# GpSimd adds the squares of the two channel groups of layer 3's output, and TensorE multiplies the mean once instead of twice

## The reference, cut to what matters

```python
x_n  = group_norm(x)                                  # 32 groups of 8 channels
q, k, v = split(silu(x_n @ w_qkv.T))
q, k = rope(rms_norm(q, w_qn)), rope(rms_norm(k, w_kn))
wp = silu(x_n @ w_wp.T + b_wp)                        # width and sharpness of the mask
scores = (q . k over the 49 neighbours) * scale - (1 - soft_mask(wp)) * 10000
out = softmax(scores) . v over the 49 neighbours
out = out / sqrt(mean(out * out, over the 256 channels) + eps) * w_on     # the change is in this mean
x = x + silu((out + v) @ w_out.T)
```

## Time and profile before

| what | value |
|---|---|
| median of three executions | 3406.79 us (3405.43 to 3414.38) |
| the profiled execution's own time | 3416.4 us |
| its span | 3414.6 us |
| TensorE (PE) busy | 3097.6 us, 91%, 38656 products |
| VectorE (DVE) busy | 2203.3 us, 65% |
| ScalarE (ACT) busy | 2053.3 us, 60% |
| GpSimd (POOL) busy | 1155.5 us, 34% |
| mean granted TensorE clock | 0.962 of full |

### The profile page before, as it was taken

How to read it: one execution, slowest core, us unless ns; L and a number is a source line. 1 busy time by engine, 2 the same in 40 slices (tenths; PEclk the granted TensorE clock), 3 DMA queues, 4 the chain that set the end, 5 groups by cost and what they waited for, 6 DMA issues and landing times. The chain is left out here.

```text
span 3414.6 us, 93918 instructions
## 1 busy us (share of the span) xinstructions
PE 3097.6 (91%) x38656; PEld 1747.5 (51%) x38656; DVE 2203.3 (65%) x5202; ACT 2053.3 (60%) x4412; POOL 1155.5 (34%) x1446
## 2 busy tenths in 40 slices
PE   6999999999965999999999968999995899999996
PEld 2333333333313555565656536777774566666664
DVE  5877878877744667677676633545543566666664
ACT  2667666766644555556555425666562677777774
POOL 3433434343311222222212202222222555555544
PEclk9999999999986999999999989999998999999998
DMA  6777788787753233323322214445443233333332
GB/s 202 158 173 161 160 182 178 145 183 161 151 131 107 67 88 84 86 69 92 79 71 68 71 49 162 148 146 164 141 137 137 82 94 106 106 108 113 115 94 80
DMA packets 286232, 413.93 MB, mean 121 GB/s; under 512 B 25952, under 2 KB 242800, under 8 KB 264816
## 3 DMA queue, kind: packets, MB, share of 16 engines
q1 hardware_dynamic: 262608, 272.15, 26.4%
q0 software_dynamic: 18432, 134.23, 19.7%
q10 hardware_dynamic: 4768, 1.55, 0.2%
HBM read 219.30 MB, written 53.81 MB: 80 GB/s over the span
## 5 line engine op out<-in xcount | busy, mean ns | idle before, releaser
L732 DVE TENSOR_TENSOR l_probs<-l_psum,l_decay 128x1024 f32<-128x1024 f32 x512 | 598.3, 1218 | 162.9 <-PE l_psum L628 152.2
L780 ACT ACTIVATE l_sizes<-l_probs 128x2048 f32<-128x2048 f32 x256 | 487.0, 1908 | 297.1 <-DVE l_probs L732 292.2
L1806 ACT ACTIVATE l_logits<-l_logits,l_low 128x100 f32<-128x100 f32 x1024 | 372.9, 366 | 229.7 <-DVE l_low L1786 228.8
L1813 POOL TENSOR_TENSOR l_logits<-l_logits,l_inv 128x400 f32<-128x400 f32 x256 | 235.1, 918 | 731.6 <-DVE l_inv L1792 730.7
L628 PE MATMUL l_psum<-l_qk 32*128 32x512 f32 x2048 | 338.7, 644 | 7.5 <-POOL l_qk L866 4.2
L881 POOL DMA_DIRECT2D l_sizes<-l_sizes x128 | 111.3, 870 | 548.7 <-ACT l_sizes L780 536.7
L1643 POOL TENSOR_TENSOR l_E<-l_E,l_causal 128x1024 f32<-128x1024 f32 x64 | 152.9, 2390 | 382.6 <-DVE l_x_act L1341 226.7
L643 PE MATMUL l_psum<-l_probs,l_V 128*32 128x512 f32 x2048 | 270.7, 600 | 1.8 <-DVE l_probs L732 1.6
L299 PE MATMUL l_psum<-l_xT,l_w_up 128*128 128x512 f32 x512 | 231.5, 606 | 9.8 <-DVE l_row_var L1399 9.7
L1748 PE MATMUL l_psum<-l_keys,l_q_blocks 128*64 128x100 f32 x4096 | 230.7, 253 | 4.2 <-issue 2.8
L2742 POOL TENSOR_SCALAR l_soft<-l_dist,l_sharp,l_border 128x100 f32<-128x100 f32 x512 | 229.5, 472 | 0.1
(11 more groups left out here) (247 smaller groups left out, 6056.7 us busy)
## 6 DMA issues: line engine op xcount, KB each, us to landing
l_sizes<-l_sizes POOLq DMA_DIRECT2D x128, 1024.0 KB, 7.6
l_V_windows<-v_image SPq DMA_DIRECT2D x512, 100.0 KB
l_V_windows<-v_padded SPq DMA_DIRECT2D x512, 100.0 KB
l_E<-rows_c SPq DMA_DIRECT2D x64, 512.0 KB, 5.8
l_xT<-y SPq DMA_DIRECT2D x24, 1024.0 KB, 5.2
y<-l_res SPq DMA_DIRECT2D x32, 512.0 KB, 3.1
l_e_everywhere<-rows_e SPq DMA_DIRECT2D x112, 128.0 KB, 5.6
l_xT<-x SPq DMA_DIRECT2D x8, 1024.0 KB, 10.9
```

Of the source, the lines that this page charges most:

```text
L732: nc.vector.tensor_tensor(probs[:, N % 2, 2 * p:2 * p + 2, :], ring.region(name).rearrange("p (a n) -> p a n", a=2), decay[:, h:h + 2, s0: ...
L780: nc.scalar.activation(sizes[:, slot(N), :, :], probs[:, N % 2, :, :], ACT.Abs).then_inc(sized, 1)
L1806: nc.scalar.activation(e, e, ACT.Exp, scale=-1.0, bias=self.low[:, N % 4, i:i + 1], accum_out=self.total[:, N % 4, i:i + 1]).then_inc(self ...
L1813: nc.gpsimd.tensor_tensor(p, p, self.inv[:, N % 4, :].unsqueeze(2).to_broadcast([P, STEP, NKEY]), ALU.mult).then_inc(self.p_ready, 1)
```

## The change

A new function on GpSimd adds the second group's squares onto the first's, in place, and counts a new semaphore `o_summed`. TensorE waits for that semaphore in place of `o_squared` and multiplies `all_mean` with the one sum. GpSimd calls it at `n == 11` behind `scale(N - 1)`, and at `n == 3` between `scale(N - 1)` and `apply`. Its loop is longer by three steps, so that the second half of the last image has its sum at `N = 131`.

```diff
@@ layer3, tensor
                 def out_mean(b, half):
                     name = ("om", b, half)
-                    pe.wait_ge(o_squared, 4 * b + 2 * half + 2)
+                    pe.wait_ge(o_summed, 2 * b + half + 1)
                     ring.may_fill(pe, name)
-                    for g in range(HALVES):
-                        i = nc.tensor.matmul(ring.region(name), all_mean[:, :], osq[:, g, :], start=(g == 0), stop=(g == 1))
-                    i.then_inc(ring.filled(name), 1)
+                    nc.tensor.matmul(ring.region(name), all_mean[:, :], osq[:, 0, :], start=True,
+                                     stop=True).then_inc(ring.filled(name), 1)
@@ layer3, gpsimd
+                def sum_of_squares(b, half):
+                    pool.wait_ge(o_squared, 4 * b + 2 * half + 2)
+                    nc.gpsimd.tensor_tensor(osq[:, 0, :], osq[:, 0, :], osq[:, 1, :], ALU.add).then_inc(o_summed, 1)
+
...
-                for N in range(B * STEPS + 1):
+                for N in range(B * STEPS + 4):
                     b, n = step_of(N)
-                    if N > 0:
+                    if 0 < N <= B * STEPS:
                         w.scale(nc, pool, N - 1)
...
                     if b + 1 < B and n == 2:
                         norm.variance(nc, pool, pstep, ring, b + 1)
+                    if n == 3 and b > 0:
+                        sum_of_squares(b - 1, 1)
+                    if n == 11 and b < B:
+                        sum_of_squares(b, 0)
                     if b + 1 < B:
                         if n == 3:
                             apply(b + 1)
```

More of the change, by code:

```diff
@@ L2238, in layer3 @@
         o_squared, or_ready, z_ready, added = L.sem("o_squared"), L.sem("or_ready"), L.sem("z_ready"), L.sem("added")
+        o_summed = L.sem("o_summed")
         stored, cleared = L.sem("stored"), L.sem("cleared")
```

## The result

The changed kernel is slower: 3440.19 us (median of seven executions, 3427.3 to 3447.93) against 3406.79 us (3396.25 to 3414.38), a ratio of 1.0078 with an interval of 1.0052 to 1.0105. In a second measurement, 3444.97 against 3416.83 us, the ratio was 1.0053 (1.0027 to 1.0079). The ratios are those of the record; the quotients of the two medians are larger, 1.0098 and 1.0082. Forecast was +7.15 us, 1.0021. Both measured intervals lie above that, and 3440.19 lies above the whole range.

The account below looks back on a forecast made before the run. Bound: GpSimd's normalisation at step 3, ScalarE at step 11, not TensorE. Terms 0 + 6.2 + 1.3 + 0.25 - 0.6 = +7.15 us took the 3406.8 us median to 3413.9 us; range 3406 to 3421.

Parts of the forecast that it names:

- the clock falls: Rival, chance 0.03: TensorE's pause at step 11 lowers its clock once an image, some +24 us, 3431 us.
- ScalarE hides it all: 0: Step 11, images 0 to 6: the mean ends 0.7 us later, within ScalarE's 1.5 us of room; cost 0.
- So this second delay costs nothing: Step 3, images 1 to 6: the mean ends 0.5 us later, still ahead of the next projection; no cost.
- `apply` behind `scale`: Step 3, GpSimd's queue: the addition delays `apply` 1.2 us in image 1, 1.0 in five others; 6.2 us.
- The loss beside VectorE: Step 3: `apply` loses 1.64 us to VectorE's query products; the addition would take part of this loss, not add to it.
- Full blocking: Rival, chance 0.17: at step 3 GpSimd and VectorE exclude each other fully; +14.6 us, 3421.4 us; sign: over 6.4 us.
- agrees in kind, not in full: Step 3: the skill's full-length exclusion of VectorE and GpSimd would cost `apply` 2.7 us; the trace showed 1.64.
- An image of 93.2 us: Expected sign: the distance from one image's `wp` projection to the next becomes 93.2 us in place of 92.2.
- Step 3 of the last image: No `apply` there; the later mean delays VectorE's next scores: +1.3 us (0.5 to 2.4).
- The last two means: Last image's end: step 11 costs +0.25 us; the last half, at the lower clock, gains 0.6 us.
- TensorE as the bound: Rival, chance 0.04: all 15.8 us of saved TensorE products count, giving 3391.0 us.
- the hidden delay: Rival, chance 0.14: later steps absorb `apply`'s delay, only the last image's terms stay; +1 us, 3407.8 us.

Follow-up runs that it names:

- e5: The change made at step 11 only, step 3 as in the kernel before: ratio 1.0014 to the kernel before, stretch 728.7 us.
- e6: The change made at step 3 only, step 11 as in the kernel before: ratio 1.0033 to the kernel before, stretch 735.4 us.
- e8: e4 with further filler products at steps 4 and 6, ahead of TensorE's waits: ratio 1.0018 to the kernel before, stretch 728.5 us.
- e4: The changed kernel with two throwaway products on TensorE ahead of its wait for the addition: ratio 1.0015 to the kernel before, stretch 729.3 us.
- e2: The kernel before with one product per mean and no addition, second group's squares left out: ratio 0.9992, stretch 726.0 us.
- e1: The changed kernel, but TensorE multiplies the sum twice at half weight: ratio 1.0099 to the kernel before, stretch 756.2 us.
- e7: The changed kernel with the addition on VectorE in place of GpSimd: ratio 1.0007 to the kernel before, stretch 724.9 us.
- e10: e7 with filler products at steps 4 and 6: ratio 1.0019 to the kernel before, stretch 722.7 us.

## Why the prediction was wrong, point by point

**The step that failed** is the rival "the clock falls", held at 0.03 because "the granted clock was 1.00 … in spite of TensorE's gaps there", and with it the two sentences that cost TensorE's later mean at nothing: "ScalarE hides it all: 0" and "So this second delay costs nothing". At the full clock both hold, as the images of e5 and e6 without falls and the chain of e8 show. But they treat an idle pause of TensorE as free if its end is not on the chain, and here the pause changes the speed of what comes behind it: granted clock 0.96 for 1.00, 11.2 to 14.3 us. At the lower level the work behind the mean takes longer than ScalarE or `apply` can cover, and the chain moves over to the addition, the mean and TensorE. The forecast had seen the pause at step 11 ("TensorE will stand still for 1.9 us", measured 1.90), priced a fall at 24 us, and named the clock among the things that would make it wrong. It did not name the same pause at step 3, 2.13 us for 0.22, though its own times put that mean 1.4 us later. The gaps that before had survived were shorter ones at these places, 0.22 us ahead of each mean; that they did no harm was no evidence for ten times as much. The one long pause of before, 1.85 us an image at the projection of the values, was harmless in its first trace and had three falls in its second, and the prediction did not look at it.

**That the fall is the cause, and not a companion,** is shown by images of one trace (in e6 93.29 and 93.47 us without falls, 94.09 and 94.06 with two), and by e4 and e8: they add work in the pause, leave the addition, its wait and the queue as they are, and the time goes down by 10.4 and 11.2 us while the clock goes from 0.96 to 0.99 and 1.00.

**The rest of the sum held at the full clock; the last image's end, at the lower level, did not.**
- The addition, 1.2 us forecast (1.04 to 1.49): 1.27 us median, 1.71 us beside the query products.
- `apply` behind `scale` 1.0 us later, in image 1 1.2 us: 1.13 and 1.14.
- The loss beside VectorE is tied to VectorE's instructions: addition and `apply` take 1.71 + 4.41 = 6.12 us, under the bound of 6.4 us, and lose 6.12 - 1.27 - 3.10 = 1.75 us to the products where `apply` alone lost 1.64. Full blocking would be 4 x 0.68 + 1.27 + 3.10 = 7.09 us; that rival's price falls (6.69 us if the 0.40 us that the products run ahead of the addition are taken off). VectorE pays as well, its four products take 4.37 us for 3.40.
- The mechanism of that rival is nearer than its price, and than the prediction's "agrees in kind, not in full". Single instructions of VectorE's timeline, the first two of the four products:

```profile
3050.76 0.98 DVE L2490 TENSOR_TENSOR l_q_blocks<-l_silu_q,l_rec 32x512 f32<-32x512 f32 x1
...
3051.76 1.66 DVE L2490 TENSOR_TENSOR l_q_blocks<-l_silu_q,l_rec 32x512 f32<-32x512 f32 x1
```

- The second stands beside the addition (3051.16 to 3052.87) and ends 0.54 us behind it, so all but 0.14 us of its own 0.68 come after the addition. The addition in turn ends 1.13 us behind the first product's end (3051.74), all but 0.14 us of its 1.27. So these instructions behave as if they excluded each other for nearly their whole length. The sum comes out below 7.09 us because the first product had begun against `scale`, and because such hand-overs overlap a little.
- An image of 93.2 us: 93.29 and 93.47 in e6 without falls, 93.35 to 93.40 in e8.
- Step 11 hidden by ScalarE: 92.19 and 92.21 us for e5's images without falls. The root stood right behind the table load in turns with a fall as well, so this sign could not tell them apart.
- Step 3 of the last image, +1.3 us: from the start of its query products to the start of the next `scale` it is 5.64 us (3334.59 to 3340.23) for 4.09 (3326.62 to 3330.71), +1.55.
- The last two means: the saving of 1.85 us was forecast for the last one, since its products ran at the lower level in the kernel before, and it is there; but now both means run at that level. The chain of the changed kernel:

```profile
3378.86 1.28 POOL l_O_square L2755
...
3380.18 2.07 PE l_psum L2369 x2
...
3403.28 2.08 PE l_psum L2369 x2
```

3.69 us have become 2.08, 1.61 less; and 1.98 have become 2.07 in place of the 1.0 forecast, so that step 11 of the last image costs some 1.4 us (1.28 + 2.07 and the hand-over, less 1.98) and not 0.25.

**The rivals.** TensorE as the bound is refuted by e2, the price of full blocking by the 6.12 us, the hidden delay by e8's images of 93.4 us. The clock rival has the right mechanism with a size of its own: 3431 us by 3 us of doubled products an image was closer than the forecast, but the falls come in some turns only, fourteen of them, and cost 1.1 and 1.7 us an image in images 1 to 5 of the two traces (94.54 and 95.15 us for e8's 93.46) and 5.5 us at the end, beside the forecast's +7 and not in its place.

**What stays open.** Which turns fall: at step 11 TensorE is busy 2.91 of 5 us ahead of the mean both where the level falls and where it does not. The kernel before isn't free of it: its first trace has no fall in the images, its second three, with 0.99. By the two ratios the whole times differ by 18 to 27 us (0.0053 and 0.0078 of 3410), by the medians by 28 to 33, the stretches by 18 to 21; what lies between may be the clock in layers 1 and 2, which differs from execution to execution with no line changed, but no run isolates it. How much of the clock's part comes from the addition's wait and how much from the missing products is not separated: e2 has seven falls in its images without the first, e1 nine without the second. And e7 and e10 leave open why the VectorE version, with 32 products less on TensorE, is not shorter at all; that the products never lay on the chain, as e2 shows, is the likeliest and was only argued for it.

## What to carry to other kernels

Before putting a second engine's work between TensorE and its input, look at how long TensorE will stand still, even where it has room: a pause that is hidden in the order of the work can come back as a lower clock on the products behind it, and then the chain moves to them. Fewer products widen such pauses too. Read the granted clock by windows before and after, and, if it has dropped, put throwaway products into the pause before judging the rest of the change: that separates the clock's part from the queue's. And an operation saved on the busiest engine is worth nothing where the chain does not pass through it: count it there first.

## What the runs showed of the hardware that was not expected

- In a TensorE that is busy 90% of the images (581.99 of 646.00 us), two further pauses of mostly 1.8 to 2.1 us an image, beside one of 1.85 us that was there, brought the granted clock of the images from 1.00 to 0.96; windows about them show 0.74 and 0.80. More work in the pauses brought it back to 1.00.
- Half the products of the mean and nothing else (e2) brought it to 0.98: the pause before `wp` grew from 7.2 to 13.1 us in seven waits.
- The level falls in some turns and not in others of like busy time (2.91 of the 5 us ahead of the mean in both).
- An addition of 128x512 on GpSimd beside VectorE's two-input products takes 1.71 us for 1.27 alone, and VectorE's four take 4.37 us for 3.40: both engines pay. The Trainium skill (SBUF — State Buffer, "Who interferes with whom") states exclusion for the whole length of an instruction. By single instructions this case's trace agrees but for 0.14 us at each of the two hand-overs read above; the sum over both engines' queues is smaller, 6.12 us for 7.09.
